# The order of TensorE's work among a mixture's experts: a turn behind the first product, the second product behind the next group's first step

## What is computed

```python
router_weights = jax.nn.softmax(xf @ rw + rb, axis=-1)
topw, topi = jax.lax.top_k(router_weights, K)          # K = 2 of E = 8
topw = jax.nn.softmax(topw, axis=-1)
h = jax.nn.gelu(jnp.einsum('td,edf->etf', xf, w1) + b1[:, None, :], approximate=False)
eo = jnp.einsum('etf,efd->etd', h, w2) + b2[:, None, :]
out = jnp.einsum('etd,te->td', eo, combine)
```

## Time and profile before

| | us |
|---|---|
| median of 3 runs (3526.52 to 3534.48) | 3531.7 |
| the profiled execution | 3552.23 |
| its span, as the profile shows it | 3550.4 |
| phase b on TensorE, first turn to the end of the last product (1642.54 to 2296.20) | 653.7 |
| of it TensorE busy | 586.6 |
| TensorE's mean granted clock over the whole execution, as a share of the full one | 0.943 |

### The profile page before, as it was taken

One profiled execution on the slowest core, in us unless ns is written; L12 is line 12 of the kernel. 1 busy time (PEld: TensorE's weight loads), 2 busy tenths in 40 slices (PEclk: granted clock), 3 DMA queues, 4 the chain that ended last, 5 costly groups with the idle time before them and its releaser, 6 DMA issues. The chain is left out here.

```text
span 3550.4 us, 61837 instructions
## 1 busy us (share of the span) xinstructions
PE 3175.3 (89%) x24016; PEld 2475.3 (70%) x24016; DVE 1568.4 (44%) x4051; ACT 1547.1 (44%) x3403; POOL 874.2 (25%) x991
## 2 busy tenths in 40 slices
PE   6999998889989999875898898869999999998996
PEld 4778776676777767654777787746677767776765
DVE  4544465435555564442100000065455656555533
ACT  3554555535545455341121121135555555554553
POOL 2121233222322233221000000052233434332322
PEclk8999999999999999876999999979999999999998
DMA  8543454444453554723556545364334645355422
GB/s 175 66 57 56 59 87 69 62 61 70 67 78 62 61 80 68 166 40 130 188 191 194 170 166 175 115 101 55 44 58 65 82 59 78 57 75 67 61 44 38
DMA packets 394607, 319.34 MB, mean 90 GB/s; under 512 B 151711, under 2 KB 378271, under 8 KB 394303
## 3 DMA queue, kind: packets, MB, share of 16 engines
q1 hardware_dynamic: 374550, 280.97, 44.4%
q0 software_dynamic: 8272, 23.73, 2.5%
q10 hardware_dynamic: 11493, 10.70, 0.9%
HBM read 134.33 MB, written 37.22 MB: 48 GB/s over the span
## 5 line engine op out<-in xcount | busy, mean ns | idle before, releaser
L1045 DVE TENSOR_REDUCE a_maxima<-a_bank 128x2 f32<-128x512 f32 (+3 forms) x576 | 344.9, 647 | 228.2 <-PE a_bank L668 219.4
L896 ACT ACTIVATE a_prob<-a_bank 128x512 f32<-128x512 f32 (+1 forms) x640 | 338.3, 601 | 176.6 <-PE a_bank L688 171.0
L932 ACT ACTIVATE b_group_hidden<-b_bank,b_b 128x256 f32<-128x256 f32 x312 | 131.0, 471 | 508.2 <-PE b_bank L754 508.2
L896 ACT ACTIVATE c_prob<-c_bank 128x512 f32<-128x512 f32 (+1 forms) x512 | 272.3, 597 | 164.0 <-PE c_bank L688 161.2
L1045 DVE TENSOR_REDUCE c_maxima<-c_bank 128x2 f32<-128x512 f32 (+2 forms) x448 | 263.8, 638 | 128.5 <-PE c_bank L668 127.8
L799 PE MATMUL a_bank<-a_causal_b,keep_identb 128*128 128x256 bf16 (+1 forms) x768 | 253.4, 330 | 63.3 <-DMA a_qs<-a_parts_q 29.5
L754 PE MATMUL b_bank<-b_group_xt,b_w 128*128 128x256 f32 x1248 | 297.8, 400 | 0.8 <-DVE b_group_xt L1086 0.8
L754 PEld LDWEIGHTS b_bank<-b_group_xt,b_w 128*128 128x128 f32 x1248 | 249.0, 202 | 37.9 <-DVE b_group_xt L1086 1.2
L738 PE MATMUL b_bank<-b_w,b_group_hidden 128*128 128x256 f32 x1248 | 273.9, 380 | 0.0
L738 PEld LDWEIGHTS b_bank<-b_w,b_group_hidden 128*128 128x128 f32 x1248 | 238.0, 191 | 32.5
L1086 DVE COPY b_group_xt<-b_bank 128x512 f32<-128x512 f32 x39 | 27.0, 692 | 340.7 <-PE b_bank L754 312.3
(11 more groups left out here) (237 smaller groups left out, 6684.3 us busy)
## 6 DMA issues: line engine op xcount, KB each, us to landing
b_w<-in_L_xattn_e_w SPq DMA_DIRECT2D x78, 1024.0 KB, 8.0
a_qs<-a_parts_q SPq DMA_DIRECT2D x384, 128.0 KB
c_qs<-c_parts_q SPq DMA_DIRECT2D x288, 128.0 KB
a_ks<-a_parts_k SPq DMA_DIRECT2D x192, 128.0 KB
c_ks<-c_parts_k SPq DMA_DIRECT2D x96, 128.0 KB
b_group_x<-sorted_in SPq DMA_DIRECT2D x39, 256.0 KB, 7.2
sorted_out<-b_group_y ACTq DMA_DIRECT2D x39, 256.0 KB, 5.5
sorted_in<-a_zeros SPq DMA_DIRECT2D x8, 1024.0 KB
```

What stands on the lines that cost most here:

```text
L896: act.activation(prob[0:rows, first:first + cols], bank[0:rows, 0, 0:cols], ACT.Exp, scale=SCALE).then_inc(k.own(s), 1)
L932: ins = act.activation(hidden[:, f, :], bank[:, 0, j * S:(j + 1) * S], ACT.Gelu, bias=b1[:, f:f + 1])
L1045: v.tensor_reduce(maxima[:, q:q + qn, h:h + n].rearrange("p q h -> p h q"), bank[:, 0, 0:cols].rearrange("p (j q n) -> p j q n", j=n, q=qn ...
```

## The change

Three `behind` entries are added in `expert_steps`; no step, wait, size or buffer is added or taken away.

```diff
-    plan.step("tensor", "group_turn", g, "b", us=0.44, after=[("group_load", g, "b")], takes=["bank"], gives=["x"], x=x, bank=bank)
+    plan.step("tensor", "group_turn", g, "b", us=0.44, after=[("group_load", g, "b")],
+              behind=[("expert", g - 1, "b", 1)] if g else [], takes=["bank"], gives=["x"], x=x, bank=bank)
...
         plan.step("tensor", "expert", g, "b", f, us=1.73,
                   after=[("group_turned", g, "b"), ("w1_load", g, "b")] + ([("expert", g, "b", f - 1)] if f else []),
+                  behind=[("expert_out", g - 1, "b")] if g and f == 1 else [],
...
     plan.step("tensor", "expert_out", g, "b", us=7.0, after=[("gelu", g, "b", FT // 2 - 1), ("w2_load", g, "b")],
+              behind=[("expert", g + 1, "b", 0)] if g + 1 < GROUPS else [],
```

## The result

| | before | after |
|---|---|---|
| median of 4 runs each, us | 3529.11 (3522.07 to 3534.48) | 3433.39 (3429.52 to 3446.99) |
| ratio to before, 95% interval | | 0.9737 (0.9703 to 0.9771) |
| the profiled execution, us | 3552.23 | 3429.83 |
| phase b on TensorE, us | 653.7 | 560.65 |

A forecast was written before the change was run, and what follows sets the result against it. TensorE was taken to bound phase b. Floor 559.3 + start 3.0 + end 1.1 = 563.4 against 653.7, −90.3 (66.1 waits, the rest clock and refills); 3531.7 − 90.3 = 3441 us, range 3428 to 3472.

The forecast's parts named there:

- The waits: Phase b, TensorE's turns: all 24 waits for group_load after the one ahead of the phase go, −66.1 us.
- The other loads: Phase b: w1 has 28.7 us and w2 36.1 to land; DMA engines' share rises from 0.53 to about 0.62.
- The clock: TensorE in phase b: ten stretches of 8.76 instead of 7.07 go, −16.9 us; clock 1.00 in the middle.
- last 10 or so: Phase b: remainder of the 94.4 us lost, put down to the cold start and the pipeline's refilling after each wait.
- the second rival: TensorE's clock doesn't hold in phase b: one slow stretch per group, 39 × 1.69 = 66, so 3507 us; 6%.
- The copy and the gelus: Phase b: one step (1.73) covers VectorE's copy of the turn and ScalarE's last gelu; cost nothing.
- The first rival: Phase b: copy or last gelu comes late once per group, 39 × 1.04 = 41, so 3482 us; 8%.
- A group: TensorE's floor per group in phase b: (14.83 + 13.82) / 2 = 14.33 us; 39 groups 558.9.
- The start and the end: Phase b: start 3.0 us over the floor, first second product near 1655; group 38's bare gelu at the end, +1.1.
- The fold: VectorE's fold, waiting for GpSimd's last load, delays a sum by some 2 us; copy has 4; cost nothing.
- The transfer to the median: Whole kernel: the profiled execution's gain of 90.3 us taken over unchanged to the median, 3531.7 − 90.3 = 3441.
- The third rival: Phase b's loads become a ring, slower than before: about 3580 us at a landing of 40; 4%, half past slower.

The follow-up runs named there:

- the two kernels with a load moved: Kernel before with group_load issued one group earlier on SP: planner free to answer, ratio 0.9988; every other engine's order kept, ratio 0.9795.
- the two kernels without a cover: Changed kernel with the turn behind part 3 (copy bare), ratio 0.9867; with each second product right behind its own group's last step (gelu bare), ratio 0.9883.

## Why the prediction was right, point by point

- **The waits.** Predicted: all 24 of them go, −66.1. Measured: all 24 gone, 84.4 to 18.2. The half with the turn's entry alone shows that it is the turn's place, the two kernels with a load moved show that it is the rows' landing. The prediction took the place from the diff and did not ask why the planner had chosen the old one: a `lag` of 4.4 for a landing of 7.2. Nor did it see that the turn's entry is without effect beside the other two.
- **The issue on SP.** Predicted 3.15 behind the product's end. In the trace after, a second product ends 6.91 behind 1703.22, at 1710.13, and the rows are issued at 1713.27, 3.14 later:

```profile
1703.22 7.07 PE L742 MATMUL b_bank<-b_w,b_group_hidden 128*128 128x256 f32 x32
...
1713.27 0.39 SPq L1341 DMA_DIRECT2D b_group_x<-sorted_in  x1
```

- **The other loads.** Predicted: not late, DMA engines busy 0.62 of the time. Measured 0.62; the rows land in 3.9, 6.8 and 10.9 us (shortest, median, longest), where they took 4.0, 7.2 and 10.7 before, and two buffers suffice.
- **The clock.** Predicted −16.9 and a clock of 1.00 in the middle. Measured: no stretch of 8.76 in the middle, 1.00. Busy time fell by 586.6 − 558.9 = 27.7, so 10.8 more than the ten stretches. These are the "last 10 or so" that the prediction named without splitting them, and the rows do split them. One part is the start before, three rows of which are:

```profile
1657.47 3.62 PE L754 MATMUL b_bank<-b_group_xt,b_w 128*128 128x256 f32 x8
...
1664.33 10.49 PE L754 MATMUL b_bank<-b_group_xt,b_w 128*128 128x256 f32 x40
...
1692.69 15.21 PE L738 MATMUL b_bank<-b_w,b_group_hidden 128*128 128x256 f32 x64
```

  At the full clock they take 1.89, 8.80 and 13.98, so 4.7 are lost, and the first step took 3.43 for 1.89, another 1.5; the change pays 1.5 at its own start. With two more turns of 1.11 for 0.66 the start is worth some 5.6. The other part is the stops: behind the wait of 3.24 the overlap of 0.16 is lost and the turn takes 0.50 instead of 0.44, so 0.22, which is about 5.3 for 24 stops.

  The Trainium skill (TensorE: Matmul & The Clock Gate, A second HAM failure mode: psum-queue depth-cycling) tells of a kernel, bf16 with an N of 512, that took another bank each time and idled between its groups of matmuls so often that its clock fell again and again. The prediction made the second rival's 3507 of it. In this order the steps go through the eight banks in turn for 560 us, at 1.00 from the fourth step on, and even the pauses of 0.78 and 0.93 of the two kernels without a cover, one in every group of 15.30 or 15.45, leave the clock in the middle at 1.00. So taking another bank did nothing to the clock by itself; how a kernel with more frequent pauses would do, no run here shows.
- **The copy and the gelus.** Predicted at nothing, with 0.9 and 0.7 to spare. Measured at nothing: 558.90 busy of 560.65, and the 1.75 idle are the first copy (0.78) and the last gelu (0.93). The first rival did not come true; its price was a little low, 41 for its dearer form, 46.5 when made real.
- **A group.** Predicted 14.33, measured 14.25. The prediction took (14.83 + 13.82) / 2, where the two turns cost 0.5 each in the earlier trace rows; in the stream a turn costs 0.44 and a step 1.725. Over 39 groups that is 3.1, and it is why phase b took 560.65 and not 563.4: the mis-sized floor outweighs a slightly dearer end.
- **The start and the end.** Predicted 3.0 and 1.1, the first second product near 12.6 behind the first turn (1655 − 1642.5). Measured 12.5. The first turn and copy take 1620.94 − 1619.04 = 1.90 for 0.44, the three steps behind them 1627.63 − 1620.94 = 6.69 for 5.18: together 3.0, as predicted. The end takes 0.93 of wait and the stop's 0.27, and the last record's 0.16 has nothing behind it to overlap with: 1.4. With 39 × 14.25 + 0.4 = 556.2 that is the 560.65. The start is partly luck: in other kernels of this study the slow part of it was 3.1 long instead of 1.5, which the prediction had allowed for ("up to 4.7").
- **The fold.** Predicted: a sum 2 late, a copy in time, no cost. In the trace after, the fold starts at 1994.05 and the sum behind it at 1995.38, 14.25 before the next sum (2009.63): not even the sum was late, and no wait of TensorE stands near it.
- **The transfer to the median.** The gain was taken over unchanged from the profiled execution: 90.3 forecast, 93.0 in phase b, 95.7 between the medians. The last 2.7 are within the spread of the phases where nothing moves, so that they are no larger is in part luck. That spread also meets the prediction's last sign of being wrong, that phase c takes another time than before: it took 5.9 less. But phase c varies by 10.4 over the eleven kernels, and the sign was set without knowing that.
- **The third rival.** With one buffer the loads bound phase b, at 922, but through `w1` as much as through the rows; with two or three they are far from it.

No better version came out of it. TensorE is busy for 558.9 of phase b's 560.65, at the full clock, with the work that the kernel gives it; another order of the same work can win no more than the 4.4 that phase b lies above 556.2.

## What to carry to other kernels

When an in-order engine waits for a load, look first at what stands behind the waiting instruction: here ready matmuls did, for a result that was needed half a pair or more later, and 66 us of waits cost 93, the slow steps at the start among them. Where a planner made the order, compare its assumed latencies with the landings in the trace before writing an order out by hand: one number, 4.4 to 7.2, brought eight to nine tenths of the gain, while moving the load up was answered by a turn that moved up with it. One step of cover is enough for a copy or a gelu on an idle engine, but each one lost costs its wait and 0.3 us more.

## What the runs showed of the hardware

- A stop of TensorE ahead of a step or a second product costs 0.27 us beyond its wait, at a granted clock of 1.00, the same behind a wait of 0.78 as behind one of 0.93. Ahead of a turn it cost 0.22 (the kernel before, behind a wait of 3.24).
- Short pauses leave the clock alone, longer ones not always: in the two kernels without a cover no wait of 0.78 or 0.93 behind the start, one in every group, is followed by a slow stretch, while in the kernel before 20 of the 24 waits were 2.2 to 4.0 long, and ten of these were followed by a stretch of 8.76 instead of 7.07, two more, near the start, by the slow rows of 10.49 and 15.21. The length alone doesn't decide it there: one of 2.17 was followed by such a stretch, one of 3.49 was not. With one buffer, where waits of 4.13 and 1.50 stand in a group, the clock was 0.81.
- A phase whose program doesn't change took 1619.0 to 1642.5 us from one execution to the next, while phase b, bound by TensorE, took 560.65, 560.71 and 562.27 with one and the same order on TensorE. Two profiled executions are compared phase by phase, not by their spans.
